# Row scatters of the second routing paced by the attention steps, their rest held for the last norm, first scatters held for landings, and one routing moved earlier

## The reference

```python
x = x + 0.5 * ffn(layernorm(x), ...)      # layer 0 of the experts
x = x + attn(layernorm(x), ...)           # 16 heads, causal
x = x + 0.5 * ffn(layernorm(x), ...)      # layer 1 of the experts, same weights

def ffn(x, ...):                          # 2048 tokens, 32 experts, 4 per token
    shared = silu(xf @ sg) * (xf @ su) @ sd
    ...                                   # scores, 4 of 8 groups, then 4 of 32 experts
    gates = softmax(top_scores)
    pos = cumsum(onehot)[...] - 1         # place of the token in its expert
    keep = pos < capacity                 # capacity 320
    buf[e, pos] = xf[token]
    out_e = silu(buf @ wg) * (buf @ wu) @ wd
    return shared + sum over 4 of gate * keep * out_e[e, pos]
```

## Time and profile before

| | |
|---|---|
| median of 3 runs | 1106.93 us (1106.89 to 1107.83) |
| the profiled execution's own time | 1111.37 us |
| its span | 1109.6 us |
| mean granted clock of TensorE | 0.95 |
| PE busy | 880.5 us, 79% of the span |
| DVE busy | 569.3 us, 51% |
| ACT busy | 393.9 us, 35% |
| POOL busy | 331.1 us, 30% |

### The profile page before, as it was taken

The page is one execution under the profiler, slowest core; times in us unless marked ns, Lnnn a source line. Parts: engine busy times, 40 slices in busy tenths (PEclk is TensorE's granted clock), DMA queues, the critical chain, the costliest instruction groups (busy, mean ns, idle before and its releaser), DMA issues.

```text
span 1109.6 us, 16209 instructions
## 1 busy us (share of the span) xinstructions
PE 880.5 (79%) x4979; PEld 715.9 (65%) x4979; DVE 569.3 (51%) x1678; ACT 393.9 (35%) x779; POOL 331.1 (30%) x327
## 2 busy tenths in 40 slices
PE   2341699989279989999999889689999938998980
PEld 1240377777237789988984778579888725777770
DVE  7540144444346677565752776266546515544453
ACT  2100122222134356464643545246435413322220
POOL 2477225555500000000000014531000352355552
PEclk9999999999779999999999999699999978999995
DMA  7950224454253010223111021311112011545535
GB/s 273 395 154 23 57 78 140 143 154 150 96 180 85 20 48 24 54 77 98 37 46 21 1 62 45 84 38 25 39 23 54 22 48 40 143 138 151 153 114 193
DMA packets 97971, 103.45 MB, mean 93 GB/s; under 512 B 14953, under 2 KB 82427, under 8 KB 97398
## 3 DMA queue, kind: packets, MB, share of 16 engines
q1 hardware_dynamic: 88694, 90.30, 27.1%
q0 software_dynamic: 9216, 12.38, 3.6%
HBM read 58.70 MB, written 42.90 MB: 92 GB/s over the span
## 4 chain that ended last, share of the span: by engine, by line
PE 57%; DVE 16%; issue 9%; DMA 8%; another core or an unknown queue 5%; SPq 3%; ACT 1%; POOL 1%; POOLq 0%; DVEq 0%; ACTq 0%
PE PS L1624 17%; PE PS L1582 6%; DMA area_v<-xbuf 6%; PE PS L1607 5%; PE PS L1503 4%; PE PS L1499 4%; DVE mxp L1180 4%; PE PS L1513 3%; PE PS L1475 2%; PE PS L1521 2%; DVE den L1243 2%; PE PS L1644 2%; PE PS L1422 2%; SPq L503 2%
## 5 line engine op out<-in xcount | busy, mean ns | idle before, releaser
L1624 PE MATMUL PS<-pT,area_v 128*128 128x256 f32 (+1 forms) x1280 | 308.6, 365 | 0.4 <-ACT pT L827 0.4
L1180 DVE TENSOR_REDUCE mxp<-PS 128x2 f32<-128x512 f32 (+1 forms) x320 | 197.0, 630 | 138.6 <-PE PS L1582 62.3
L827 ACT ACTIVATE pT<-PS 128x512 f32<-128x512 f32 (+1 forms) x320 | 176.5, 553 | 235.7 <-PE PS L1610 109.7
L1624 PEld LDWEIGHTS PS<-pT,area_v 128*128 128x128 f32 x1280 | 215.6, 196 | 15.4 <-ACT pT L827 0.8
L663 POOL DMA_INDIRECT ybuf<-area_o,yidx x160 | 155.4, 972 | 173.6 <-DVE area_o L1147 131.1
L1582 PE MATMUL PS<-Kz,Qx 128*128 128x256 f32 (+1 forms) x640 | 168.3, 355 | 20.9 <-DVE mxp L1180 13.2
L649 POOL TENSOR_TENSOR area_o<-area_o,rden 128x512 f32<-128x512 f32 x31 | 39.5, 1274 | 481.3 <-DMA rden<-den 480.7
L619 POOL DMA_INDIRECT xbuf<-xn,sidx x128 | 125.4, 980 | 103.3 <-issue 56.3
L1607 PE MATMUL PS<-Qx,Kz 128*128 128x256 f32 (+1 forms) x640 | 144.6, 308 | 4.6 <-issue 2.2
L1582 PEld LDWEIGHTS PS<-Kz,Qx 128*128 128x128 f32 x640 | 113.5, 196 | 44.4 <-DVE mxp L1180 19.2
L1607 PEld LDWEIGHTS PS<-Qx,Kz 128*128 128x128 f32 x640 | 103.4, 197 | 8.6 <-issue 3.8
(11 more groups left out here) (181 smaller groups left out, 859.7 us busy)
## 6 DMA issues: line engine op xcount, KB each, us to landing
area_v<-xbuf SPq DMA_DIRECT2D x32, 342.5 KB
ybuf<-Kz SPq DMA_DIRECT2D x4, 2048.0 KB
area_v<-in_L_ffn_wg_dram SPq DMA_DIRECT2D x32, 256.0 KB
area_v<-in_L_ffn_wu_dram SPq DMA_DIRECT2D x32, 256.0 KB
area_v<-in_L_ffn_wd_dram SPq DMA_DIRECT2D x64, 128.0 KB
rden<-den SPq DMA_DIRECT2D x248, 32.0 KB
yg<-ybuf SPq DMA_DIRECT2D x12, 512.0 KB, 4.7
qkbuf<-stage SPq DMA_DIRECT2D x24, 256.0 KB, 3.6
```

Source lines behind the costliest of these rows:

```text
L827: nc.scalar.activation(pT[:, N % 4, 0:w], PS[:, 2 + N % 2, 0:w], ACT.Exp).then_inc(exp_done, 1)
L1180: nc.vector.tensor_reduce(mxp[:, i, c, 2 * hp:2 * hp + 2], PS[:, k % 2, 0:2 * w].rearrange("p (h w) -> p h w", h=2), AX.X, ALU.max).then_i ...
L1624: ins = mm(PS[:, pv_bank(U, a), (p + 1) * TC - w:(p + 1) * TC], value_and_ones(j, h), pT[:, N % 4, a * w:(a + 1) * w], start=(N in UNIT_FI ...
```

## The change

Four edits:

- Layer 1's first 32 scatters stand at every other step, 194 to 256, and each waits until the exponent before its step is done (`exp_done`). The wait also stands before the scatters at `SCAT_LAST`.
- `SCAT_LAST` is steps 304 to 317: 14 scatters. The other 18 wait for `last_norm`; the last 8 of them wait for piece 5 as before.
- Layer 0's tiles 1, 2 and 3 each wait until all scatters before them have landed.
- The routing of piece 4 moves: scores from step 299 to 294, groups 301 to 295, experts 303 to 297, the one-hot rows and the gates' exponent 305 to 299, counts and slots 307 to 302.

```diff
-S_STAT, S_ROWS, S_TURN, S_SCORE = [O_STEPS[0] + k for k in (14, 16, 17, 27)]
-S_GROUP, S_EXP, S_HOT, S_GATE, S_COUNT = [O_STEPS[0] + k for k in (29, 31, 33, 33, 35)]
+S_STAT, S_ROWS, S_TURN, S_SCORE = [O_STEPS[0] + k for k in (14, 16, 17, 22)]
+S_GROUP, S_EXP, S_HOT, S_GATE, S_COUNT = [O_STEPS[0] + k for k in (23, 25, 27, 27, 30)]
...
-SCAT_STEPS = list(range(FIRST[V_C] + 10, FIRST[V_C] + 10 + K * HT))
-SCAT_LAST = list(range(S_COUNT + 2, len(STEPS) + 5))
+SCAT_STEPS = list(range(FIRST[V_C] + 10, FIRST[V_C] + 10 + 2 * K * HT, 2))
+SCAT_LAST = list(range(S_COUNT + 2, len(STEPS) - 2))
...
                 for t in range(lo, hi):
+                    if H == 0 and 0 < t < HT // 2:
+                        pool.wait_ge(scat, 16 * K * t)
                     for k in range(K):
                         scatter_one(L, H, t, k)
...
                         tk = steps.index(step)
+                        pool.wait_ge(exp_done, step)
                         scatter_one(1, H, tk // K, tk % K)
...
+            pool.wait_ge(last_norm, 1)
             for tk in range(len(SCAT_LAST), K * HT):
                 scatter_one(1, 1, tk // K, tk % K)
```

## The result

The changed kernel takes **1090.5 us** (median of four runs, 1084.4 to 1093.4), the kernel before 1107.1 beside it: ratio 0.983, 95% interval 0.981 to 0.986. The forecast was 1071 in a range of 1056 to 1092: the sign and the range hold, the gain is 17 us where 36 were named. The profiled execution is the fastest of the four (1084.4, span 1082.6), 27 us under that of before (1111.4); for the other three, 4 to 9 us slower, there is no trace.

A forecast was written before the change was run, and what follows sets the result against it. Long scatter bunches were taken to stall engines in batch 1's attention, the attention's end and the start. -20 - 12 - 4 = -36 us on the profiled 1111.4 gives 1075.4; the median, 4.4 lower, 1071 us; range 1056 to 1092.

The forecast's parts named there:

- the scatters are not the cause: Rival, chance 0.04: the waits in all three places have another origin, spacing changes nothing; 1107 to 1112 us.
- The middle, -20: Batch 1's attention: one scatter every other step costs nothing; 16.8 us gained in one visit, 3.7 in the visit before.
- (n - 2) x 1.1: Rule from batch 1's attention: us lost by a bunch of n back-to-back scatters; 2.2, 6.6 and 11 for 4, 8, 12.
- The end, -12: Attention's end and behind it: sum -21 + 4 + 5 - 3 + 3 us, bounds -29 and +7.
- (a): Attention's end: today's ACT and DVE waits up to the last norm go, as no scatter runs there; -21 us.
- (b): Steps 304 to 317: the 14 paced scatters start as a bunch that breaks; +4 us, upper bound 13.
- (c): From the last norm: ten held scatters beside `last_part` may freeze the engines; +5 us, bounds 0 and 9.
- (d): Steps before 304: piece 4's earlier routing delays maxima on DVE, +6; later steps shed waits, 3; net +3 us.
- The clock's -3: Behind the last norm: without PE's idle time, part of the low-clock loss is given back; -3 us, at most 5.
- The start, -4: Layer 0's front: three landing waits mostly covered by POOL's idle time, DVE's slots earlier; -4 us, bounds -12 and +5.
- 10.94 us in which POOL sits idle: Start, behind the first 16 scatters: POOL's gap until DVE's next slots, taken to cover three waits of 0.9 us.
- the front opens: Rival, chance 0.07: in the start, POOL's pauses end DVE's freezing and shorten PE's slow stretch; 1055 us.

The follow-up runs named there:

- mid_only_again: Kernel before with only the 32 scatters of batch 1 at every other step, each waiting for its exponent, on a stalling chip: 1081.8 us, ratio 0.9855.
- mid_untied_again: Kernel before with only the 32 scatters of batch 1 at every other step, no wait on exponents, on a stalling chip: 1083.2 us, ratio 0.9871.
- routing_only: Kernel before with only piece 4's routing moved up, so paced scatters begin five steps earlier and none is held, on a stalling chip: 1106.6 us, ratio 1.0082.
- mid_undone: Changed kernel with the 32 scatters of batch 1 at every step again and not tied to exponents, on a calm chip: 1030.1 us, ratio 1.0325.
- before_again: The kernel before, unedited, run again for a profile, on a calm chip: 998.8 us, ratio 1.0000.

## Why the prediction came out as it did

**What bounds the kernel.** Scatters as the cause of the waits in three places: for the middle shown by `mid_only_again` and `mid_untied_again`, on chips that stall like that of the forecast. For the end it rests on `routing_only`, where the stall moves with the run, for the start on the change itself, whose only edit there breaks up the first 16. For the 48 scatters behind them, under which PE's slow stretch lies, no run on a stalling chip tests it. The coincidence had one thing missing from it, that the same runs leave another chip alone (`mid_undone`, `before_again`). The rival "the scatters are not the cause" fell on chips like that of the forecast.

**The middle, -20.** Measured: visits 5 to 7 go from 39.0 + 54.0 + 55.1 to 37.6 + 35.2 + 56.4 us, -19. The size is right, partly by luck; the picture behind it was not. Visit 5 gave 1.4 us where 3.7 were named, visit 6 gave 18.8 where 16.8 were (it takes 34.5 without stalls, not the 37.2 taken from another visit), and visit 7 lost 1.3. The text expected singles 2.8 us apart; there are bunches of 4 and 5, for which its rule (n - 2) x 1.1 gives 2.2 and 3.3 each. They cost 0.7 to 1.2 (the two runs of six in `mid_untied_again` 2.1 and 1.6). The 4, 8 and 12 of before had only a `scale` between them, no pause: read again, they are one long run, and the rule took its three parts for three sizes.

**The end, -12.** This is the sum that failed: -3 from visit 9 to the first result of layer 1. It can be split because the same code runs without stalls on chip 9, and the kernel before on chip 1.
- (a) losses of today, -21: before, visit 10 and the stretch behind it take 21.1 + 67.9 us, without stalls 18.8 + 51.0, so 19 of stall. Right.
- (b) the paced ones, +4: visit 10 takes 25.2 us against 16.4 without stalls, +9. This step failed in size: "POOL waits too and the bunch breaks" did not come true, since GpSimd was late and found the exponents of all but the last scatter over. Three bunches of 4 were taken where one of eleven came; the text's own upper bound, 13, was the nearer.
- (c) the held ten, +5: behind the last exponent 52.8 us against 49.8 without stalls, +3.
- (d) the routing moved, +3: visit 9 +7.8 for +6 taken, visit 10 without stalls 16.4 for 18.8, so -2.4 for -3 taken: +5. Mis-sized by VectorE's idle time in visit 9, which is less than the text hoped for.
- The clock's -3 did not show apart: without stalls the stretch behind the last exponent is 1.2 us shorter, from all parts of the change together.

In sum -19 + 9 + 3 + 5 - 1 = -3.

**The start, -4.** Measured -3.5 at the first exponent, a number that came out right by luck. The way forward for pieces 1 and 2 was right and stronger than named: with the first 16 scatters broken up VectorE's slots come 11 us earlier (42.3 and 58.1, as without stalls: 42.6 and 58.5), and PE does 27.2 us of work up to 73 instead of 16.5. So the bound at which "PE's fold is over before the slow stretch" was met, and PE's tiny products did not come 2.8 us apart as foretold. Against it stand the waits, 6.3 to 9.6 us each, above the 5.3 of the bound: the last scatter starts 12.6 us later. Of PE's work 21.1 us are left from there to the first result scatter instead of 34.2, so that this comes 2.3 us earlier, at 155.3 instead of 157.6. Even that is not clearly the change's: in the four traces of the other stalling chips, whose front is that of before, it comes at 155.6 to 156.2, and the first exponent at 338.8 to 340.4, earlier than the 341.5 here.

The "10.94 us in which POOL sits idle" were no slack of the program: VectorE was late there because it was stalled. Without stalls GpSimd issues all 64 without a gap, and every wait goes straight into the time, 25 us in all. The rival "the front opens" came for the fold alone; under the long run of scatters PE's slow stretch stayed.

**The sum.** -19 for the middle, -3 for the end, -6 for the start (3.5 and another 2.3 in visit 0, whose 65.5 or 63.2 us are found in stalling and calm traces, with either kernel's code there), +1 behind: -27, that of the profiled executions. The median of the runs gained 10 less than that pair. No run or trace here says where the slower executions of the changed kernel lose it; that stays open.

**The rule against the change.** The Trainium skill, "SBUF — State Buffer", "Who interferes with whom", by which PE and ACT never wait on anyone and no DMA contends with a compute engine, fits chips 1, 4 and 9: runs of eleven and twelve scatters leave no such waits there (visit 6 of `before_again` takes 34.5 us). On the four others the waits are real (5.61 us in the earlier trace rows), and in the middle they fall when the run is broken up. By the equal durations of the instructions it isn't their access to memory that suffers, but what starts the next one. That last point is argued from the rows; no run isolated it.

## What to carry to other kernels

Before tuning around a wait whose cause reads "remote" or "issue", run the unchanged kernel on a second and a third chip: here 108 of 1107 us were there on one chip and not on another, and a change fitted to them gained 1.7% on the one and lost 2.9% on the other. Slack read in a stalled stretch is not slack; a wait placed there is paid in full wherever the stall is absent. Of a bundle of edits keep the one that gains where it can and costs nothing elsewhere: the thinner list, without the waits, the hold and the early routing.

## What the runs showed of the hardware

- The same program takes 998.7 to 999.0 us on chips 1, 4 and 9 and 1095.6 to 1097.6 on chips 6, 10 and 11 (1107 on that of the forecast), each run within 0.6% of its chip's median. Whether this goes with the chip or with the hour can't be told: each was used in one session only. Among the stalling ones it differs by degree, by 12 us in time.
- On the second kind PE, VectorE and ScalarE are held up under runs of indirect DMAs issued by GpSimd, 1.28 us apart: ScalarE waited 6.05 us behind eleven in a row, and an exponent was about 1 us late behind four or five with a pause before them. The experts' results, 16 groups of five scatters in a layer, take 132 to 137 us there instead of 117.9, about 1 us a group; that these scatters are the cause there too is not shown.
- The instructions' own durations don't change (553 and 554 ns an exponent), nor does GpSimd's rate (1.28 us a scatter). What holds the engines up stays open.
- A wait for the landing of four scatters held GpSimd 6.3 to 11.2 us in the start, on both kinds of chip.
